# Attention kernel on one core: the band mask of pair 0 copied into PSUM by ScalarE in 17 of 20 slots

## The reference

```python
band = jnp.abs(idx[:, None] - idx[None, :]) <= WINDOW // 2      # WINDOW = 128
mask = jnp.where(band, 0.0, -jnp.inf)
scores = jnp.einsum('bhqd,bhkd->bhqk', q, k) * SCALE + mask      # H = 16, HD = 16
attn = jax.nn.softmax(scores, axis=-1)
out = jnp.einsum('bhqk,bhkd->bhqd', attn, v)
```

## Time and profile before

| | before |
|---|---|
| median of 3 runs | 974.45 us (972.28 to 976.3) |
| profiled execution | 980.85 us |
| its span | 979.1 us |
| PE busy | 728.8 us (74%) |
| DVE busy | 509.6 us (52%) |
| ACT busy | 402.7 us (41%) |
| POOL busy | 507.6 us (52%) |

### The profile page before, as it was taken

How to read it: one execution, slowest core, us unless ns; L and a number is a source line. 1 busy time by engine, 2 the same in 40 slices (tenths; PEclk the granted TensorE clock), 3 DMA queues, 4 the chain that set the end, 5 groups by cost and what they waited for, 6 DMA issues and landing times.

```text
span 979.1 us, 15496 instructions
## 1 busy us (share of the span) xinstructions
PE 728.8 (74%) x4789; PEld 477.4 (49%) x4816; DVE 509.6 (52%) x1976; ACT 402.7 (41%) x883; POOL 507.6 (52%) x514
## 2 busy tenths in 40 slices
PE   5679999989888988988987775200999988888200
PEld 3335556455454554554563443100888777676100
DVE  3176669678689678577676664500222221222038
ACT  3236665555555555565543341000444343433100
POOL 5000011256375474464555656776488888887730
PEclk9879999899999998998998976555999999999655
DMA  8684998366455464464344449201999998889877
GB/s 303 176 329 146 318 339 248 117 203 219 169 194 201 156 229 142 161 201 148 106 155 145 148 139 276 80 26 34 251 276 279 264 219 163 155 166 190 202 227 320
DMA packets 165262, 191.47 MB, mean 196 GB/s; under 512 B 21753, under 2 KB 146709, under 8 KB 165180
## 3 DMA queue, kind: packets, MB, share of 16 engines
q1 hardware_dynamic: 128764, 134.14, 42.8%
q0 software_dynamic: 30720, 38.03, 18.9%
q10 hardware_dynamic: 5696, 18.30, 4.9%
HBM read 100.64 MB, written 110.67 MB: 216 GB/s over the span
## 4 chain that ended last, share of the span: by engine, by line
PE 36%; DVE 21%; issue 14%; POOL 12%; DMA 10%; ACT 4%; another core or an unknown queue 1%; ACTq 1%; POOLq 0%; DVEq 0%; SPq 0%
DMA acc_d<-ys,xg 8%; POOL acc_d L737 6%; DVE junk L1297 5%; PE stageA L990 4%; POOL slots_d L661 4%; PE scores L1024 4%; PE outT L1066 4%; PE scoresT L1240 4%; PE stageA L1006 3%; PE scoresT L1046 3%; PE scoresT L1050 3%; PE stageC L1107 2%; DVE sc L1395 1%; PE turns L1076 1%; PE stageC L1125 1%
## 5 line engine op out<-in xcount | busy, mean ns | idle before, releaser
L661 POOL DMA_INDIRECT slots_d<-H,dest x256 | 257.8, 1007 | 206.3 <-PE outT L1066 73.6
L1297 DVE CUSTOM_DVE_ANT_0 junk<-scores,mask 128x256 bf16<-128x256 f32 x512 | 188.1, 420 | 102.3 <-PE scores L1024 58.1
L737 POOL DMA_INDIRECT acc_d<-ys,xg x128 | 198.2, 1548 | 60.3 <-issue 29.6
L798 ACT ACTIVATE PT<-scoresT 128x512 f32<-128x512 f32 (+1 forms) x320 | 154.2, 513 | 99.8 <-PE scoresT L1050 79.6
L1240 PE MATMUL scoresT<-xgT,wgu 128*128 128x256 f32 x512 | 127.8, 393 | 23.1 <-ACT xgT L903 23.1
L1046 PE MATMUL scoresT<-mask,identb 128*128 128x512 bf16 (+1 forms) x320 | 113.8, 356 | 17.1 <-ACT PT L798 9.9
L1240 PEld LDWEIGHTS scoresT<-xgT,wgu 128*128 128x128 f32 x512 | 96.0, 194 | 48.3 <-ACT xgT L903 35.1
L1024 PE MATMUL scores<-Ks,Qs 96*128 96x256 bf16 x512 | 103.2, 285 | 17.9 <-DVE mrowmax L1297 12.8
L1050 PE MATMUL scoresT<-Qs,Ks 98*128 98x256 bf16 (+1 forms) x640 | 113.8, 260 | 0.0
L1066 PE MATMUL outT<-PT,Va 128*32 128x256 f32 (+1 forms) x1280 | 91.5, 358 | 6.6 <-ACT parts L780 3.4
L1050 PEld LDWEIGHTS scoresT<-Qs,Ks 98*128 98x128 bf16 x640 | 65.5, 102 | 39.5 <-issue 10.0
(11 more groups left out here) (225 smaller groups left out, 1115.8 us busy)
## 6 DMA issues: line engine op xcount, KB each, us to landing
xg<-slots_d SPq DMA_DIRECT2D x64, 324.0 KB
slots_d<-blank ACTq DMA_DIRECT2D x26, 648.0 KB, 5.7
parts_d<-parts SPq DMA_DIRECT2D x32, 384.0 KB, 3.9
Qs<-parts_d SPq DMA_DIRECT2D x96, 128.0 KB
Ks<-parts_d SPq DMA_DIRECT2D x90, 128.0 KB
acc_d<-zero SPq DMA_DIRECT2D x32, 272.0 KB
wgu<-L_ffn_w_gate_dram SPq DMA_DIRECT2D x64, 128.0 KB
wgu<-L_ffn_w_up_dram SPq DMA_DIRECT2D x64, 128.0 KB
```

The lines of the kernel that those rows point to most:

```text
L661: pool.indirect_dma_start(out=slots_d[:, :], in_=H2[bt.par][:, t, :], in_offset=None, out_offset=bass.IndirectOffsetOnAxis(ap=dest[bt.par] ...
L737: pool.indirect_dma_start(out=acc_d[ACC[e]][:, :], in_=ys[e % NY][:, h, :], in_offset=None, out_offset=bass.IndirectOffsetOnAxis(ap=xg[e % ...
L798: sc_.activation(PT[m % NPT][:, :, 0:w], src, ACT.Exp).then_inc(sems["exp"], 1)
L1297: ins = v.tensor_tensor_reduce(out=junk[:, i, :], in0=bS[n % 2][:, i * 2 * P:(i + 1) * 2 * P], in1=mask[:, edge, :], scale=1.0, scalar=TAK ...
```

## The change

In 17 of 20 slots (LAID; not in 3, 8 and 16) the mask of pair 0 is put into bST[0] by an ACT copy. The copy for a slot is issued on ACT right behind the two exponentials of the slot before, ahead of the other steps of that slot; the copy for slot 0 of a batch stands behind slot 19 of the batch before, and the very first one ahead of the loop, behind take_mT. It counts up a new semaphore, laid. On PE, pair 0 of such a slot has no mask product: it waits for exp as before, then for laid, and goes on with the K and Q products, which are unchanged (start=False). Pair 1, and pair 0 of slots 3, 8 and 16, keep their mask products.

```diff
+    laid=17, ...
+LAID = (0, 1, 2, 4, 5, 6, 7, 9, 10, 11, 12, 13, 14, 15, 17, 18, 19)

+        def band(u):
+            half = mask[:, 1, P:2 * P] if u == 0 else mask[:, 1, 0:P] if u == U - 1 else mask[:, 1, :]
+            return half.unsqueeze(1).to_broadcast([P, 2, P if u in (0, U - 1) else 2 * P])
+        def masks_laid(slots):
+            return sum(s < slots for s in LAID)

 # ACT
+            def lay_mask(bt, slot):
+                if slot not in LAID:
+                    return
+                u = slot % U
+                w = P if u in (0, U - 1) else 2 * P
+                after(act, "exp", bt, 2 * slot - 1)
+                sc_.activation(bST[0][:, 0:2 * w].rearrange("p (h q) -> p h q", h=2), band(u), ACT.Copy
+                               ).then_inc(sems["laid"], 1)
                     exps(now, g, u, 0)
                     exps(now, g, u, 1)
+                    if slot < SLOTS - 1:
+                        lay_mask(now, slot + 1)
+                    elif nxt:
+                        lay_mask(nxt, 0)
                     if u == 2 and (g < QUADS - 1 or nxt):
                         take_mT(*((now, g + 1) if g < QUADS - 1 else (nxt, 0)))
 ...
             take_mT(batch(0), 0)
+            act.wait_ge(s_v1, 3)
+            lay_mask(batch(0), 0)
             batches(body)

 # PE, scoresT
                 after(pe, "exp", bt, m - 1)
-                half = mask[:, 1, P:2 * P] if u == 0 else mask[:, 1, 0:P] if u == U - 1 else mask[:, 1, :]
-                mm(bST[m % 2][:, 0:2 * (hi - lo)].rearrange("p (h q) -> p h q", h=2), identb[:],
-                   half.unsqueeze(1).to_broadcast([P, 2, hi - lo]), start=True, stop=False, skip_group_check=True)
+                if p == 0 and U * g + u in LAID:
+                    after(pe, "laid", bt, masks_laid(U * g + u + 1))
+                else:
+                    mm(bST[m % 2][:, 0:2 * (hi - lo)].rearrange("p (h q) -> p h q", h=2), identb[:], band(u),
+                       start=True, stop=False, skip_group_check=True)
```

More of the change, by code:

```diff
@@ L63 @@
     exp=10 * QUADS, pv=10 * QUADS, oTs=QUADS, oTp=QUADS, rec=QUADS, on=QUADS,
-    onTp=C, onT=C, op=2, t1=2, x1=2, xs=1, stats2=T, aggr2=T, rstd2=8, xn2=T, h2=4, h2Tp=C, h2T=C,
+    laid=17, onTp=C, onT=C, op=2, t1=2, x1=2, xs=1, stats2=T, aggr2=T, rstd2=8, xn2=T, h2=4, h2Tp=C, h2T=C,
     lg=1, ex=1, route=38, pre=T + 1, idc=1, cntp=1, key=2, near=T,
```

## The result

The change makes the kernel slower. The ratio to the kernel before is 1.012, 95% interval 1.0097 to 1.0143. It leaves out runs that took over 1.5% more than the fastest of their kernel, 6 of 20 for the changed kernel, while the medians over all runs are 988.95 and 974.33 us. Beside two further sets of runs of the kernel before the ratio was 1.013 (1.0092 to 1.0167) and 1.0136 (1.0095 to 1.0177). So the change loses 12 to 13 us. On the 974.45 us of the prediction 1.012 makes 986 and 1.0136 makes 988: the upper end of the stated range (966 to 988), outside the likeliest case (975 to 982), and three times the forecast of +4.

What follows compares the result with a forecast made beforehand. Attention was taken as a chain changing hands between PE and DVE, PE alone bounding only batch 0. Batch terms +0.8, +0.9, +1.5 and about +1 made +4.2, rounded to +4: 974.45 + 4 = 978.5 us, range 966 to 988.

Steps and rivals of the forecast that it cites:

- likeliest case: Whole kernel: late copies nearly balance removed products, about +1 to +7 us, 975 to 982 us; chance 0.43.
- What is removed: PE, 17 slots a batch: pair 0's mask products go, 2.86 us a batch, 22.9 us over eight batches at full clock.
- What is added: 136 ACT copies into PSUM priced like exponentials (596 and 389 ns), 54.6 us more ACT work, one more PE wait per slot.
- rival 1: Copy into PSUM 0.2 us shorter, so late slots shrink: -4 to -8 us, 968 us; chance 0.24.
- The rule for a late slot: First K product starts at pair 1 exponential's end - 0.10 + copy (0.60 or 0.39) + 0.14 release; 50 of 135 slots late.
- Batch 1: Slots 4 and 9 late, 0.35 + 0.75, hT +0.4, less removed products in slots 10 to 14: net +0.9 us.
- Batches 2 to 6: Slots 4 and 10 late, 0.35 + 0.46, less 0.22 and 0.3 for products: +0.3 us each, +1.5 together.
- Batch 0: All on PE: 11 slots in time give 1.8 us, 6 late cost 1.7, ACT pushback about 0.9: net +0.8.
- Slot 7: Copy late by 0.33 us, hidden in front of the 1.32 us in which PE waits for DVE anyway.
- Rival 3: Emptier PE loses clock in slots 13 to 16: one more dip in four batches, +13 us, about 991; chance 0.11.
- Rival 2: ACT's queue decides, every late slot is passed on: +12 us, 986 us; chance 0.19.
- the remote wait: Slot 9, batches 2 to 6: ACT idles 2.13 us for a cause called remote, hiding the slot's 0.75 us lateness.

Runs made afterwards that it cites:

- x3: Kernel before without pair 0's mask product in the 17 slots, no copy, no new wait, scores unmasked; 1.0002 of the kernel before.
- x2: Kernel before plus the 136 ACT copies into a spare SBUF tile, all mask products kept, no new wait; 1.0049 of the kernel before.
- x9: The changed kernel once more, on a third chip, against the kernel before on that chip; 1.0136 of its time.
- x10: The change in slots 4, 9 and 10 alone (24 copies), against the kernel before; 1.005 of its time.
- x1: The changed kernel run again, against the kernel before on the same chip; 1.013 of its time.
- x4: Copies and waits as in the changed kernel, but PE still makes its mask product over the copy; 1.0147 of the kernel before.

## Why the prediction came out as it did

- **What is removed.** Right as a quantity of PE time (0.22 and 0.11 us a product, 2.86 a batch). Of these batch 1 sees 1.0 us at full clock (x3). That most of it does not shorten the batch was the reading of the earlier trace rows, and it holds there.
- **What is added.** Right. The copy takes 605 and 396 ns. The Trainium skill's figures (ScalarE: Activation LUTs, what ACT_TABLE_LOAD costs) gave 613 and 399, and the trace agrees within 8 ns. That PSUM is the lower-latency destination, as the Trainium skill has it (ScalarE: Activation LUTs, Step-by-step: what each stage is for), the traces bear out: x2's copies into SBUF take 629 and 423 ns, 24 and 27 more. That is a tenth of the 0.2 us of rival 1, the quick copy, which is out.
- **The rule for a late slot.** Right to 0.02 us. Slot 4 of batch 0: 69.05 + 1.06 + 0.43 = 70.54, found 70.52. Slot 9 of batch 1, in x9, PE and ACT:

```profile
148.78 0.27 PE L1080 MATMUL scoresT<-Qs,Ks 98*128 98x128 bf16 x2 [0.99 <-ACT scoresT L819]
```

```profile
147.30 1.07 ACT L810 ACTIVATE PT<-scoresT 128x512 f32<-128x512 f32 x2
148.25 0.39 ACT L819 ACTIVATE scoresT<-mask 128x256 f32<-128x256 bf16 x1
```

 147.30 + 1.07 + 0.43 = 148.80, found 148.78. In 69 of the 136 slots the K product starts within 0.3 us of the copy's end (median 0.14), where the rule had 50 late. What a late start costs the batch is another matter: in batches 2 to 5 of x10 slot 4 costs 0.34 of its 0.35, slots 8 to 10 at most 0.2 of the 0.46 put down for slot 10.
- **Batch 1**: forecast +0.9, found 0.0 to +0.7 (x9, x1). The waits were as forecast, the relief was larger than the 0.33 + 0.3 written for it.
- **Batches 2 to 6**: forecast +0.3 each. In x9 they are +0.1, +3.2, +1.3, +5.4 and -0.7. This is the term that was mis-sized, +1.5 for the five and 9.3 found in x9, 5.0 in x1. What it lacks is the clock: the sum took the clock of the kernel before as given. The surplus comes with 10.2 to 13.7 us at half clock in batches 3 to 5, against 0 to 6.8 before. Part of it can be the new waits in slot 13 instead; no run separates the two.
- **Batch 0**: forecast +0.8, found +2.6 and +3.2. Slot 4 is late by 0.7 as written, and in x9 it then runs at half clock, 1.4 us more.
- **Slot 7**, late by 0.3, was put down as hidden in front of PE's wait for DVE. Its lateness is hidden, but it is where the clock falls in batches 3 to 6 of x9, 1.7 us each.
- **Rival 3** (0.11) named this mechanism, at +13 us for four dips on top of the forecast. Its place was slots 13 to 16; in x9 the new falls are in slots 1 and 7. Found: about 40 us more at half clock, for 9 to 10 us by the estimate above. It deserved more than a chance of 0.11, since removing products could give little in those slots but could cost the clock everywhere.
- **Rival 2** (0.19) priced the copies and waits by themselves at +12. x4 measures +14.4 for them, but the removed products would pay 9 us of this at full clock, an estimate. Its point of decision, the remote wait in slot 9, was not what decided: in x10 this wait takes the lateness up, and in batch 1 of x9, without such a wait, slot 9 began 0.73 us later behind slot 8 and the batch was no longer.

The forecast's mechanism, late copies against removed products near balance, held in batch 1. Over the kernel the balance was missed by 8 to 9 us. In the terms of the sum, late slots and queue came to about 9 us and the relief to about 5. Measured were 14.4 (x4) and nothing (x3); the comparison is rough, since the sum counts the product of a late slot with its lateness. The range held the result only because it reached to rival 2's price, which is no merit of the sum.

## What to carry to other kernels

Where PE and another engine take turns on the chain, products taken off PE are worth only what they shorten on the chain, here a third (1.0 of 2.86 us a batch); the rest makes PE emptier, and the emptier PE lost clock: with 0.02 less of mean clock, all the relief was gone. A step handed to another engine inherits that engine's queue: read the end of whatever stands in front of it, add the step and the release (0.14 us here), and compare with when the consumer used to start; slots in which this comes out late should keep the old way. And look at the granted clock of both kernels before giving a reason for a small loss.

## What was not expected of the hardware

- The kernel before takes 978 us on two chips and 955 us on a third (974 beside the result). The missing 23 us go with waits whose releaser the profile cannot name (13.0 us on ACT, 15.5 on DVE in the lines above). On the slower chips they stand from batch 2 on, mostly in slots 9, 10, 13 and 16 and not in the same ones in every kernel; in the four profiles of the faster chip they are all but absent. Their cause stays open.
- Adding 72 idempotent products to the kernel before lifted its mean clock from 0.888 to 0.901 and its speed by 0.7% on the chip without these waits.
- The runs of the changed kernel that the ratio counts spread from 977 to 991 us (the kernel before: 969 to 978), with the mean clock from 0.878 down to 0.857; on the whole, the lower the clock, the longer the run.
- A copy of a bf16 mask by ACT is 24 to 27 ns shorter into PSUM (605 and 396 ns, x9) than into SBUF (629 and 423 ns, x2).
